# Second layer: who adds up the experts' outputs, GpSimd or VectorE

## The reference, cut to what matters

```
def _L1_ffn_ref(x, W_gate, b_gate, W_e, b_e):
    TOP_K = 2
    logits = x @ W_gate + b_gate
    _, top_idx = jax.lax.top_k(logits, TOP_K)
    y_all = jax.nn.relu(jnp.einsum('bsd,edh->bseh', x, W_e) + b_e)
    y = jnp.take_along_axis(y_all, top_idx[..., None], axis=2)
    return y.mean(axis=2)
...
x = x + _L1_ffn_ref(_layernorm(x, axis=-1), L1_ffn_W_gate, L1_ffn_b_gate, L1_ffn_W_e, L1_ffn_b_e)
```

## Time and profile before

| | us |
|---|---|
| median of 3 runs | 1885.27 (1885.04 to 1886.22) |
| the profiled execution | 1885.55 |
| its span in the trace | 1883.8 |
| TensorE busy | 1781.2 (95%) |
| VectorE busy | 1236.2 (66%) |
| ScalarE busy | 900.6 (48%) |
| GpSimd busy | 495.4 (26%) |

### The profile page before, as it was taken

One profiled execution on the slowest core, in us unless ns is written; L12 is line 12 of the kernel. 1 busy time (PEld: TensorE's weight loads), 2 busy tenths in 40 slices (PEclk: granted clock), 3 DMA queues, 4 the chain that ended last, 5 costly groups with the idle time before them and its releaser, 6 DMA issues. The chain is left out here.

```text
span 1883.8 us, 36264 instructions
## 1 busy us (share of the span) xinstructions
PE 1781.2 (95%) x14128; PEld 983.3 (52%) x14128; DVE 1236.2 (66%) x2288; ACT 900.6 (48%) x1433; POOL 495.4 (26%) x370
## 2 busy tenths in 40 slices
PE   5989999999999999999999999977999999999997
PEld 2545555555555555555555444443555555555553
DVE  6785565646565646566566577758777877877863
ACT  5544444343434343434444333243666666666662
POOL 0161832505207034076000000000223322322324
PEclk9989999999999999999999999989999999999999
DMA  5011220301204012034100300004100000000000
GB/s 229 23 45 46 86 95 23 124 2 69 79 1 143 4 47 101 1 112 147 57 2 1 118 1 1 0 11 170 51 7 7 7 13 7 7 13 7 7 12 12
DMA packets 18376, 88.79 MB, mean 47 GB/s; under 512 B 2608, under 2 KB 2864, under 8 KB 10160
## 3 DMA queue, kind: packets, MB, share of 16 engines
q1 hardware_dynamic: 18224, 86.58, 12.7%
HBM read 65.60 MB, written 20.97 MB: 46 GB/s over the span
## 5 line engine op out<-in xcount | busy, mean ns | idle before, releaser
L642 PE MATMUL bank<-R 128*128 128x512 f16 (+1 forms) x7152 | 1304.7, 341 | 23.7 <-issue 7.1
L642 PEld LDWEIGHTS bank<-R 128*128 128x128 f16 x7152 | 584.4, 99 | 659.7 <-issue 40.9
L1490 DVE SCALAR_TENSOR_TENSOR R<-bank,biases,R 128x512 f16<-128x512 f32 x288 | 204.6, 746 | 249.8 <-ACT R L1095 209.0
L505 POOL TENSOR_TENSOR R<-R 128x512 f32<-128x512 f32 x112 | 156.2, 1395 | 430.2 <-ACT R L1286 428.9
L1095 ACT ACTIVATE R<-bank,biases 128x512 f16<-128x512 f32 x128 | 87.7, 686 | 235.2 <-PE bank L642 234.5
L396 POOL TENSOR_SCALAR R<-R 128x2048 f32<-128x2048 f32 (+1 forms) x20 | 33.8, 1692 | 435.9 <-PE bank L642 377.2
L1286 ACT ACTIVATE R<-R,msk 128x512 f32<-128x512 f32 x128 | 90.5, 717 | 49.3 <-DVE R L1824 49.3
L1502 DVE SCALAR_TENSOR_TENSOR R<-bank,R 64x512 f16<-64x512 f32 x64 | 44.0, 688 | 100.2 <-ACT R L1103 99.7
L1575 DVE SCALAR_TENSOR_TENSOR X<-bank,X 128x512 f32<-128x512 f32 x128 | 86.8, 683 | 34.7 <-PE bank L642 34.6
L642 PE MATMUL bank<-CT,R 128*128 128x512 f16 x384 | 91.6, 390 | 17.1 <-DVE CT L1464 11.8
L1824 DVE SCALAR_TENSOR_TENSOR R<-bank,R 128x512 f32<-128x512 f32 x128 | 87.1, 681 | 29.3 <-PE bank L642 28.3
(11 more groups left out here) (148 smaller groups left out, 2022.4 us busy)
## 6 DMA issues: line engine op xcount, KB each, us to landing
R<-in_wB SPq DMA_DIRECT2D x16, 1024.0 KB, 6.0
R<-in_wX SPq DMA_DIRECT2D x16, 1024.0 KB, 5.0
w_split<-AW SPq DMA_DIRECT2D x16, 1024.0 KB, 4.8
R<-w_split SPq DMA_DIRECT2D x12, 1024.0 KB, 7.2
R<-in_ctxT SPq DMA_DIRECT2D x4, 1024.0 KB, 10.0
X<-in_x SPq DMA_DIRECT2D x4, 1024.0 KB, 13.6
out<-X SPq DMA_DIRECT2D x16, 256.0 KB, 2.4
R<-in_wB SPq DMA_DIRECT2D x7, 512.0 KB, 5.6
```

What stands on the lines that cost most here:

```text
L505: g.tensor_tensor(acc, acc, tmp[:, e % 2, :], ALU.add).then_inc(e_acc, 1)
L642: last = pe.matmul(dst, a(sa), b(sb_), start=(k == 0), stop=(k == m - 1))
L1490: v.scalar_tensor_tensor(out=dst, in0=src, scalar=bias, in1=hi, op0=ALU.add, op1=ALU.subtract).then_inc(done, 1)
```

## The change

GpSimd's loop over the tiles is removed. The same eight additions per tile become instructions of VectorE. The sum of expert e-1 (`accumulate`) comes just behind the bias of expert e, for e from 2 to 7. The sum of expert 7 and the addition onto X (`add_experts`) come behind the second `less_max` of the step, ahead of `mask_of`. The semaphores are the same, and the same two engines wait on them at the same values.

```diff
--- before.py
+++ after.py
@@ -495,23 +495,6 @@
             g.memset(REST.qs[:, :, 3, :], 0.0).then_inc(z_ready, 1)
             pool.wait_ge(z_ready, 3)
             g.memset(REST.V[64:P, :, 1, :], 0.0).then_inc(z_ready, 1)
-
-            def add_experts(n):
-
-                for e in range(1, NE):
-                    pool.wait_ge(e_rel, n * NE + e + 1)
-                    if e > 1:
-                        pool.wait_ge(e_acc, n * (NE - 1) + e - 1)
-                    g.tensor_tensor(acc, acc, tmp[:, e % 2, :], ALU.add).then_inc(e_acc, 1)
-                pool.wait_ge(e_acc, n * (NE - 1) + NE - 1)
-                xt = X[:, ds(n, 1), :].rearrange("p a d -> p (a d)")
-                g.tensor_tensor(xt, xt, acc, ALU.add).then_inc(x_done, 1)
-
-            add_experts(0)
-            with pool.Fori(1, NT) as n:
-                add_experts(n)
-
-
 
 
         def newton(dve, s, k, n, sem_r0, sem_a, sem_a2, sem_b, sem_r):
@@ -1823,6 +1806,19 @@
                     w(dve, e_acc, n * (NE - 1))
                 v.scalar_tensor_tensor(out=tmp[:, e % 2, :], in0=banks[2 + e % 2], scalar=UN, in1=beb[:, e, :],
                                        op0=ALU.mult, op1=ALU.add).then_inc(e_bias, 1)
+                if e > 1:
+                    accumulate(n, e - 1)
+
+            def accumulate(n, e):
+                dve.wait_ge(e_rel, n * NE + e + 1)
+                if e > 1:
+                    dve.wait_ge(e_acc, n * (NE - 1) + e - 1)
+                v.tensor_tensor(acc, acc, tmp[:, e % 2, :], ALU.add).then_inc(e_acc, 1)
+
+            def add_experts(n):
+                accumulate(n, NE - 1)
+                dve.wait_ge(e_acc, n * (NE - 1) + NE - 1)
+                v.tensor_tensor(x_tile(n), x_tile(n), acc, ALU.add).then_inc(x_done, 1)
 
             def q_lo(n):
                 pl = home(n)
@@ -1910,6 +1906,8 @@
                 if two:
                     expert(n - 2, 7)
                 less_max(n, 1)
+                if two:
+                    add_experts(n - 2)
                 if one:
                     mask_of(n - 1)
                 row_sums(n, 1)
@@ -2020,9 +2018,11 @@
             ffn_lo(NT - 1)
             for e in (5, 6, 7):
                 expert(NT - 2, e)
+            add_experts(NT - 2)
             mask_of(NT - 1)
             for e in range(NE):
                 expert(NT - 1, e)
+            add_experts(NT - 1)
 
 
 def kernel(**inputs):
```

## The result

| | before | after |
|---|---|---|
| median of four runs, us | 1885.74 (1885.04 to 1887.30) | 1926.49 (1926.06 to 1929.03) |
| ratio to before, 95% interval | | 1.0218 (1.0200 to 1.0235) |
| span of the profiled execution, us | 1883.8 | 1924.3 |

The change makes the kernel 40.7 us slower, 2.2%. 1932 was predicted, with 1904 to 1945 as the range.

The account below looks back on a forecast made before the run. TensorE was taken as the bound, held up by VectorE's run without idle time. 14 steps at 3.4 us (47.6) less 1.0 at the end gave +46.6 on 1885.55, so 1932 us; range 1904 to 1945.

Parts of the forecast that it names:

- the three points named: Where TensorE hangs on VectorE's run: turn_p(n, 0) on probs_lo, next tile's turn on mask_of, weigh_v(n, 1) on ScalarE's turned_p.
- the second pause: New TensorE pause ahead of the next tile's turn, waiting for mask_of's first instruction; 1.5 us a step.
- steps 1 to 6: Running shifts along VectorE's run from expert 4's bias to mask_of's first instruction, 0.65 us per addition between others.
- Step 2 of the shifts: Sum of expert 4 behind expert 5's bias on VectorE: ffn_lo and expert 6's bias come 1.30 us later.
- Step 4, the refund: probs_lo 0.88 us shorter without GpSimd adding; it ends 1.47 later and TensorE's pause before turn_p(n, 0) grows by that.
- Step 6: Sum of expert 7 (0.83) and addition onto X (0.65) ahead of mask_of: its first instruction comes 3.60 us later.
- The third pause: TensorE ahead of weigh_v(n, 1), behind expert 1's bias and ScalarE's turned_p(n, 1): 0.45 us more a step.
- The two additions costed at nothing, and the end: Sums of experts 1 and 2 hidden in VectorE's idle time; the program's end 1.3 us faster, taken as 1.0.
- The clock: Rival: TensorE's pauses halve its clock for one matmul group each step, 38 us more, 1970; chance 0.05.
- Faster: Rival: additions fit VectorE's idle time and the 0.83 us pause before turn_p(n, 0) goes; 1873; chance 0.06.
- partial: Rival: only the pause before turn_p(n, 0) counts, 1.47 us a step, mask_of having slack; 1905; chance 0.10.
- longer-waits: Rival: VectorE and ScalarE wait for each other by turns, a step 4.7 us longer; about 1950; chance 0.04.

Follow-up runs that it names:

- e1: The changed kernel with the sum of expert 7 and the addition onto X moved behind mask_of on VectorE; 1930.4 us, ratio to before 1.0234.
- e2: The changed kernel with VectorE's sum of expert 5 moved from ahead of the row sums to behind probs_lo(n, 0); 1928.5 us, ratio to before 1.0223.
- e10: The changed kernel with add_experts behind probs_lo(n, 1) and ScalarE's relus of experts 0 and 1 behind turned_p(n, 1); 1910.8 us, ratio to before 1.0136.
- e4: The changed kernel with the sum of expert 4 over one column instead of 512; 1927.0 us, ratio to before 1.0218.
- e6: The kernel before with GpSimd's seven sums over one column instead of 512; 1874.9 us, ratio to before 0.9948.
- e3: The changed kernel with the sums of experts 1 and 2 over one column instead of 512; 1927.9 us, ratio to before 1.0223.
- e5: The changed kernel with the sums of experts 3, 4, 5 and 6 over one column instead of 512; 1904.6 us, ratio to before 1.0108.
- e9: e8 with expert 7's bias between the second less_max's halves, its relu ahead of turned_p(n, 0), GpSimd's addition onto X held until probs_lo(n, 1) is done; 1879.5 us.
- e11: e9 with ScalarE's relus of experts 0 and 1 moved behind turned_p(n, 1); 1876.1 us, ratio to before 0.9952.
- e7: The kernel before with expert 6's bias behind probs_lo(n, 0) and its relu behind ScalarE's store of the turned tile; 1892.8 us, ratio 1.0044.
- e8: e7 with expert 7's bias behind the second less_max, its relu behind turned_p(n, 0), TensorE's expert 0 waiting only for its own bank's bias; 1885.2 us.

## Why the prediction was right, and where its sizes were off

The span grew by 40.5 us against 46.6 in the sum. From `scores(2, 0)` to `scores(15, 0)`, thirteen steps, in the kernel before and after:

```profile
1349.68:1812.70 463.02, 451.34 (x4162) 254.95 (x4162) 355.67 (x745) 311.00 (x505) 144.87 (x104) 1.00 0.03 9
```

```profile
1348.84:1851.24 502.40, 462.32 (x4161) 256.88 (x4161) 392.79 (x849) 313.55 (x505) 0.00 (x0) 0.98 0.02 8
```

That is 39.4 us for thirteen steps; the sum had 13 x 3.4 = 44.2. The mechanism and the direction were right, and the sum was 6.1 us too high.

- *What bounds the stage.* Right. TensorE was the bound, VectorE's average hid the run, and of the three points named, the last, `weigh_v(n, 1)` through ScalarE's `turned_p`, carries the full shift. The two others cost nothing of their own: in e1 the second pause went and the step stayed, in e2 the first fell from 2.14 to 1.03 and the step by 0.39 only. e10 shows that moving the load off that chain brings 1.7 us a step. That any new pause of TensorE lengthens the program one for one was too strong, by the same two runs.
- *The price of an addition (steps 1 to 6).* A little too high: 0.65 taken, 0.60 measured (the sum at 1542.92, the next instruction at 1543.52). The sum of expert 7 was taken at 0.83 up to the addition onto X and measured at that (1557.01 to 1557.84); the addition onto X itself was taken at 0.65 and measured at 0.61. At the end of the run a step was put at +3.42 and measures +3.17; of the 0.25, 0.09 came up to the row sums, 0.07 at the refund, 0.05 with the sum of expert 6 and 0.04 with the addition onto X.
- *Step 2 of the shifts.* The sum of expert 4 was charged 0.65. e4 shows that it costs nothing, since the wait for ScalarE's relu behind it ends at the same moment. The shift at the row sums (+2.35 forecast, +2.26 measured: 1550.80 - 1542.31 against 1534.77 - 1528.54) was right all the same, as the wait was computed from the relu's end.
- *Step 4, the refund.* 0.88 forecast; 2.03 from start to start became 1.08, so 0.95. e6 confirms the cause. TensorE's first pause grew by 1.31 (1.47 forecast).
- *Step 6.* +3.60 forecast for mask_of's first instruction, +3.35 measured. The third pause, 0.45 forecast, is 0.24 by the distances between TensorE's rows.
- *The sum over the steps.* I added 3.4 to all steps alike. Two steps of the kernel before (36.85 and 35.89 us) had pauses of TensorE at the start of a turn of its loop, for which the profile shows nothing that it waited for. After the change, the same steps are 38.67 like all others: such a pause is swallowed when VectorE is the later one. That is 1.7 us that the sum missed. With 14 x 0.23 = 3.2 and 0.8 that lies ahead of the stretch, unrelated to the change, it makes 5.7 of the 6.1.
- *The two additions costed at nothing, and the end.* Right, by e3 and by the rows of the end.
- *The clock.* I gave the rival 0.05 and held a kept clock in 1854 to 1858 against it. The clock does fall, in 5 of 13 steps, and with it one of my signs of being wrong came true (a granted clock under 1.00 in the steps; it is 0.98 over the thirteen). That it cost nothing in them was luck: the second pause hid it, and I had not counted on that. Had the change left less slack, as e2 and e10 did, it would have added some 7 us, to about 1933, which is still in the range. The rival's own price, one group at half clock in every step and 38 us, was far too high.
- *Faster, partial and longer-waits rivals.* The refund is as large as taken, and with GpSimd's sums short the time falls by 10.8 us in all (e6); the additions ahead of probs_lo outweigh it. The partial case fell with the second and third points of the run being real. The longer waits did not come: the one wait for ScalarE is 0.42.

What stays open: why the clock falls in some steps and not in others with the same pauses. The runs show only that pauses of about 2 us precede it, and that in e5, whose steps have no pause above 1.1 us, the clock stayed at 1.00 in all thirteen. In the kernel after the steps are strictly every third one (1360, 1476, 1592, 1708, 1824), in e10 they are the 2nd, 4th, 7th, 10th and 11th, and I have no experiment on it. Open too is what each part of e9 is worth: it moved a bias, a relu and an addition at once.

## What to carry to other kernels

An engine that is busy for 79% of a step, as VectorE after the change (30.43 of 38.68 us), can be the one that sets it: look for its unbroken run between two points that the bound engine waits at, and price a moved instruction by whether it lands in that run and whether a wait behind it swallows it. A pause of the bound engine is where it meets such a run, not the cost itself, so removing a pause without shortening the run brings nothing. Where GpSimd and VectorE share data in SBUF, first try to put GpSimd's work beside VectorE's instructions that read PSUM: here, with ScalarE's order changed too, that gave a step as short as with GpSimd's sums nearly gone (34.87, e11 and e6), for no added work.

## What the runs showed of the hardware

- GpSimd's additions hold up small VectorE instructions too: L1807, eight columns, took 1.25 us for 0.23 (e7), and L1812 1.11 for 0.17 (e8). In e7 the instruction ended when GpSimd's did.
- The granted clock fell to the lower level behind pauses of TensorE of about 2 us, in steps in which it worked for 35 of 37 to 39 us: 2.14 us in the kernel after and in e10, 2.06 in e2 (behind one of 1.03). Twelve matmuls then took up to 4.44 us instead of 2.75. Within one run, the same pause was followed by the fall in some steps and not in others. With pauses of at most 1.1 us (e5) it did not fall in any of the thirteen steps.
- A VectorE addition over one column takes 0.06 to 0.08 us of VectorE's time from start to start, though its own duration is 0.15; one over 512 columns takes 0.60, with a duration of 0.68.
